# Layer 0's capacity search: seven thresholds tried in one step a turn, in place of three steps of one bit

## The reference

```python
t = B * S                                        # 4096 tokens
probs = softmax(xf @ Wr)                         # 8 experts
topk_probs, topk_experts = top_k(probs, 2)
cap = ceil(t * 2 * 1.25 / 8)                     # 1280
for e in range(8):
    mask = topk_experts == e
    gate = sum(where(mask, topk_probs, 0.0), axis=-1)
    g_masked = where(any(mask, axis=-1), gate, -inf)
    vals, idx = top_k(g_masked, cap)
    g = where(isfinite(vals), vals, 0.0)
    xe = xf[idx]
    y = y.at[idx].add(g[:, None] * (relu(xe @ W1[e]) @ W2[e]))
```

## Time and profile before

| | |
|---|---|
| median of 3 runs | 1777.34 us |
| lowest, highest | 1774.52, 1782.87 us |
| profiled execution | 1775.63 us (span 1773.8 us) |
| TensorE busy, of the span | 1483.0 us (84%), granted clock 0.931 in the mean |
| VectorE busy | 1146.6 us (65%) |
| ScalarE busy | 865.4 us (49%) |
| GpSimd busy | 444.3 us (25%) |

### The profile page before, as it was taken

One profiled execution on the slowest core, in us unless ns is written; L12 is line 12 of the kernel. 1 busy time (PEld: TensorE's weight loads), 2 busy tenths in 40 slices (PEclk: granted clock), 3 DMA queues, 4 the chain that ended last, 5 costly groups with the idle time before them and its releaser, 6 DMA issues.

```text
span 1773.8 us, 40676 instructions
## 1 busy us (share of the span) xinstructions
PE 1483.0 (84%) x11707; PEld 931.5 (53%) x11707; DVE 1146.6 (65%) x3266; ACT 865.4 (49%) x1971; POOL 444.3 (25%) x542
## 2 busy tenths in 40 slices
PE   5355889999998959999995678899999699999997
PEld 4112556666565447778884245455554255555554
DVE  6733566667566847666666456566667577777775
ACT  1012344444443524434441146566665268888787
POOL 3465223223222202222321532112223200000000
PEclk9996899999899969999996589899999789999999
DMA  8442354544443422223320234344442011111110
GB/s 262 129 137 61 106 150 133 180 126 144 145 150 100 123 89 103 96 97 143 132 108 21 98 105 120 96 136 139 139 139 76 23 50 52 51 50 47 47 48 16
DMA packets 127886, 184.90 MB, mean 104 GB/s; under 512 B 14656, under 2 KB 107216, under 8 KB 125344
## 3 DMA queue, kind: packets, MB, share of 16 engines
q1 hardware_dynamic: 94864, 144.54, 25.6%
q10 hardware_dynamic: 26112, 25.17, 4.8%
q0 software_dynamic: 6816, 14.02, 2.2%
HBM read 148.44 MB, written 42.84 MB: 108 GB/s over the span
## 4 chain that ended last, share of the span: by engine, by line
PE 55%; DVE 16%; issue 13%; DMA 6%; ACT 4%; SPq 2%; POOL 2%; another core or an unknown queue 1%; DVEq 1%; ACTq 0%; POOLq 0%
PE pO L777 7%; PE pT_ L634 7%; PE pH L568 6%; PE pH L660 6%; PE pY L668 5%; PE pY L581 5%; DVE mx L1411 3%; PE pS L720 3%; PE pS L742 3%; DMA stk<-packed_qk 2%; ACT pex L894 2%; PE pT_ L632 2%; DVE ob L1507 1%; SPq L1652 1%; DVE wb L1450 1%
## 5 line engine op out<-in xcount | busy, mean ns | idle before, releaser
L894 ACT ACTIVATE pex<-pT_ 128x512 f32<-128x512 f32 (+1 forms) x768 | 427.3, 560 | 485.3 <-PE pT_ L634 306.4
L1411 DVE TENSOR_REDUCE mx<-pS 128x2 f32<-128x512 f32 x512 | 347.8, 689 | 156.3 <-PE pS L611 90.3
L634 PE MATMUL pT_<-stk 32*128 32x256 f16 x1024 | 201.0, 282 | 92.0 <-DMA stk<-packed_qk 31.6
L948 POOL DMA_INDIRECT home_y<-ysb,home x117 | 115.0, 983 | 541.2 <-DVE ysb L1434 281.6
L611 PE MATMUL pS<-stk 32*128 32x256 f16 x1024 | 207.4, 290 | 28.2 <-DVEq L1154 17.5
L777 PE MATMUL pO<-pex,va 128*9 128x256 f32 (+1 forms) x3072 | 201.7, 383 | 2.6 <-ACT pex L894 2.6
L634 PEld LDWEIGHTS pT_<-stk 32*128 32x128 f16 x1024 | 55.5, 93 | 207.7 <-issue 88.4
L887 ACT ACTIVATE wb<-pH,b 128x256 f32<-128x256 f32 x256 | 107.3, 470 | 117.4 <-PE pH L568 117.0
L581 PE MATMUL pY<-wb,w 128*128 128x256 f32 x512 | 131.7, 393 | 12.8 <-DVE wb L1450 12.8
L568 PE MATMUL pH<-XT,w 128*128 128x256 f32 (+1 forms) x512 | 133.1, 388 | 1.0
L660 PE MATMUL pH<-xsT,wb 128*128 128x128 f32 x888 | 132.2, 294 | 0.3 <-ACT xsT L863 0.3
(11 more groups left out here) (226 smaller groups left out, 2548.4 us busy)
## 6 DMA issues: line engine op xcount, KB each, us to landing
wb<-in_w SPq DMA_DIRECT2D x72, 514.0 KB
stk<-packed_qk ACTq DMA_DIRECT2D x96, 256.0 KB, 2.7
wb<-in_w SPq DMA_DIRECT2D x39, 578.0 KB
packed_qk<-qk SPq DMA_DIRECT2D x144, 128.0 KB, 2.0
wb<-gates_turned SPq DMA_DIRECT2D x8, 2048.0 KB, 7.1
pex<-gates_turned SPq DMA_DIRECT2D x8, 2048.0 KB, 7.5
xsb<-sorted_x SPq DMA_DIRECT2D x111, 64.5 KB, 4.1
sorted_x<-in_c_places SPq DMA_DIRECT2D x4, 1548.0 KB, 15.1
```

The lines of the kernel that those rows point to most:

```text
L634: return pe.matmul(bank[:, part * T:(part + 1) * T], key, stk[rows, side, j, 0:T], start=True, stop=True)
L894: ins = act.activation(pex[:, k % 8, 0:n], bank[:, 0:n], ACT.Exp)
L948: pool.indirect_dma_start(YH, bass.IndirectOffsetOnAxis(ap=home[:, place_:place_ + 1], axis=0), ysb[:, place_, :], None).then_inc(sem(f"ho ...
L1411: ins = dve.tensor_reduce(mx[:, :, j, col], bank.rearrange("p (c n) -> p c n", c=2), AX.X, ALU.max)
```

## The change

Each search step now tries seven thresholds in all experts at once, which settles three bits, and a turn does one step instead of three. The number of turns stays 10. The product C stands at step 0 only and sums 56 columns. At step 1 the number of thresholds that are reached is added up and the threshold raised; at step 3 the seven increments are divided by 8 and the next candidates made; at steps 12, 13 and 14 two, two and three of the seven are compared and counted (512, 512 and 768 elements), in the scratch tile `ra`. Every VectorE instruction of the search but the last reduce is now linked, that is waited for at once. Two uses of the S ring a turn are gone. The constant `bitf` has 56 columns instead of 8. `start_search` counts for seven thresholds as well.

```diff
-SEARCH_STEPS, SEARCHES_A_TURN, MARKS_A_SEARCH = 5, 3, 6
-SEARCH_TURNS = range(2, 12)
+SEARCHES, TRIED = SEARCH_BITS // 3, 7
+TRIED_AT_ONCE = (slice(0, 2), slice(2, 4), slice(4, 7))
+SEARCH_AT = {0: ("C", 0), 1: ("c", 1), 3: ("c", 2), 12: ("c", 3), 13: ("c", 4), 14: ("c", 5)}
+MARKS_A_SEARCH = 12
+SEARCH_TURNS = range(2, 2 + SEARCHES)
...
-            if layer == 0 and n in SEARCH_TURNS and h < SEARCHES_A_TURN * SEARCH_STEPS:
-
-                k, part = divmod(h, SEARCH_STEPS)
-                frame += [("c", 10 * k + part) if part else ("C", k)]
+            if layer == 0 and n in SEARCH_TURNS and h in SEARCH_AT:
+                frame += [SEARCH_AT[h]]
...
-        cand = sb("cand", [P, 8], I32)
-        bitf = sb("bitf", [P, 8])
-        biti = sb("biti", [P, 8], I32)
+        cand = sb("cand", [P, TRIED, 8], I32)
+        bitf = sb("bitf", [P, TRIED, 8])
+        biti = sb("biti", [P, TRIED, 8], I32)
         addb = sb("addb", [P, 8], I32)
+        above = sb("above", [P, TRIED, 8])
+        taken = sb("taken", [P, 8])
+        tried = sb("tried", [P, TRIED, 8])
+        cmpt = ra[:, :, :].rearrange("p t e -> p (t e)").rearrange("p (c e t) -> p c e t", c=3, e=8)
...
-                        first = SEARCHES_A_TURN * SEARCH_TURNS[0] - 1
-                        pe.wait_ge(sem("counted"), PRIMED + turn.count(SEARCHES_A_TURN, k - first))
-                        pe.matmul(bank[:, 0:8], onesm[:, :], cnt[:, :], start=True, stop=True)\
-                          .then_inc(s("S_full"), 1)
+                        pe.wait_ge(sem("counted"), PRIMED + turn.count(1, 1 - SEARCH_TURNS[0]))
+                        pe.matmul(bank[:, 0:TRIED * 8], onesm[:, :], tried[:, :, :].rearrange("p c e -> p (c e)"),
+                                  start=True, stop=True).then_inc(s("S_full"), 1)
...
-                chain.link(dve.tensor_copy(biti[:, :], bitf[:, :]))
-                for part in count_parts(chain):
-                    m = part()
-                    if isinstance(m, int):
-                        chain.wait(m)
-
-            def search_parts(c):
-
-                return [
-
-                    lambda bank: c.mark(dve.scalar_tensor_tensor(addb[:, :], bank[:, 0:8], float(CAP), bitf[:, :],
-                                                                 ALU.is_ge, ALU.mult)),
-                    lambda: c.mark(dve.tensor_tensor(thr[:, :], thr[:, :], addb[:, :], ALU.bitwise_or)),
-                    lambda: c.mark(dve.tensor_scalar(bitf[:, :], bitf[:, :], 0.5, None, ALU.mult)),
-                    lambda: c.mark(dve.tensor_copy(biti[:, :], bitf[:, :])),
-                ] + count_parts(c)
-
-            def count_parts(c):
-
-                return [
-                    lambda: c.mark(dve.tensor_tensor(cand[:, :], thr[:, :], biti[:, :], ALU.bitwise_or)),
-                    lambda: c.mark(dve.tensor_tensor(cmp_[:, :, :], key[:, :, :], e_t(cand[:, :].bitcast(F32)), ALU.is_ge)),
-                    lambda: dve.tensor_reduce(cnt[:, :], cmp_[:, :, :], AX.X, ALU.add).then_inc(sem("counted"), 1),
-                ]
-
-            def search(turn, tc, k, bank, s):
-
-                parts = search_parts(tc)
-                if bank is not None:
-                    searched[:] = [parts[0](bank)]
-                    tc.wait(searched[0])
-                    dve.sem_inc(s("S_free"), 1)
-                    return
-                for part in {1: (1, 2), 2: (3,), 3: (4,), 4: (5, 6)}[k]:
-                    if part != 2:
-                        tc.wait(searched[-1])
-                    searched.append(parts[part]())
-
-            searched = []
+                next_thresholds(chain)
+                for part in range(len(TRIED_AT_ONCE)):
+                    count_tried(chain, part)
+
+            def raise_thresholds(c):
+
+                c.link(dve.tensor_reduce(taken[:, :], above[:, :, :].rearrange("p c e -> p e c"), AX.X, ALU.add))
+                c.link(dve.tensor_tensor(addb[:, :], taken[:, :], bitf[:, 0, :], ALU.mult))
+                c.link(dve.tensor_tensor(thr[:, :], thr[:, :], addb[:, :], ALU.bitwise_or))
+
+            def next_thresholds(c):
+
+                c.link(dve.tensor_copy(biti[:, :, :], bitf[:, :, :]))
+                c.link(dve.tensor_tensor(cand[:, :, :], biti[:, :, :], thr[:, None, :].to_broadcast([P, TRIED, 8]),
+                                         ALU.bitwise_or))
+
+            def count_tried(c, part):
+
+                some = TRIED_AT_ONCE[part]
+                n = some.stop - some.start
+                c.link(dve.tensor_tensor(cmpt[:, 0:n, :, :], key[:, None, :, :].to_broadcast([P, n, 8, NT]),
+                                         cand[:, some, :, None].bitcast(F32).to_broadcast([P, n, 8, NT]), ALU.is_ge))
+                ins = dve.tensor_reduce(tried[:, some, :], cmpt[:, 0:n, :, :], AX.X, ALU.add)
+                if part < len(TRIED_AT_ONCE) - 1:
+                    c.link(ins)
+                else:
+                    ins.then_inc(sem("counted"), 1)
...
-                        search(turn, tc, 0, bank, s)
+                        tc.link(dve.tensor_scalar(above[:, :, :].rearrange("p c e -> p (c e)"), bank[:, 0:TRIED * 8],
+                                                  float(CAP), None, ALU.is_ge))
+                        dve.sem_inc(s("S_free"), 1)
+                    elif kind == "c" and k == 1:
+                        raise_thresholds(tc)
+                    elif kind == "c" and k == 2:
+                        tc.link(dve.tensor_scalar(bitf[:, :, :], bitf[:, :, :], 0.125, None, ALU.mult))
+                        next_thresholds(tc)
                     elif kind == "c":
-                        search(turn, tc, k % 10, None, s)
+                        count_tried(tc, k - 3)
...
-    c["c_bitf"] = np.full((P, 8), 2.0 ** (SEARCH_BITS - 1), f)
+    steps = 2.0 ** (SEARCH_BITS - 3) * np.arange(1, TRIED + 1, dtype=f)
+    c["c_bitf"] = np.broadcast_to(steps[:, None], (P, TRIED, 8)).astype(f)
```

More of the change, by code:

```diff
@@ L454, in build @@
                        (tri[:, :], d["c_tri"]), (rope0[:, :, :], d["c_rope0"]),
-                       (rope2[:, :, :], d["c_rope2"]), (bitf[:, :], d["c_bitf"]), (blockno[:, :], d["c_blockno"])],
+                       (rope2[:, :, :], d["c_rope2"]), (bitf[:, :, :], d["c_bitf"]), (blockno[:, :], d["c_blockno"])],
             "ld_1": [(wr[1][:, :], d["wr1"]), (br[1][:, :], d["br1"].partition_broadcast(P)),
@@ L672, in take_turn @@
                     elif kind == "C":
-                        first = SEARCHES_A_TURN * SEARCH_TURNS[0] - 1
-                        pe.wait_ge(sem("counted"), PRIMED + turn.count(SEARCHES_A_TURN, k - first))
-                        pe.matmul(bank[:, 0:8], onesm[:, :], cnt[:, :], start=True, stop=True)\
-                          .then_inc(s("S_full"), 1)
+                        pe.wait_ge(sem("counted"), PRIMED + turn.count(1, 1 - SEARCH_TURNS[0]))
+                        pe.matmul(bank[:, 0:TRIED * 8], onesm[:, :], tried[:, :, :].rearrange("p c e -> p (c e)"),
+                                  start=True, stop=True).then_inc(s("S_full"), 1)
                     elif kind == "U":
-                        pe.wait_ge(sem("counted"), PRIMED + SEARCH_BITS + (2 if k == 0 else 3))
+                        pe.wait_ge(sem("counted"), PRIMED + SEARCHES + (2 if k == 0 else 3))
                         equal = cmp_[:, :, :].rearrange("p e t -> p (e t)")
@@ L1257, in above_capacity @@
             def above_capacity():
-                dve.wait_ge(sem("counted"), PRIMED + SEARCH_BITS + 1)
+                dve.wait_ge(sem("counted"), PRIMED + SEARCHES + 1)
                 chain.link(dve.tensor_tensor(keep[:, :, :], key[:, :, :], e_t(thr[:, :].bitcast(F32)), ALU.is_gt))
@@ L1524, in take_turn @@
                 if l == 0 and turn.n == LOOPS[0][0] - 1:
-                    tc.pad(SEARCHES_A_TURN * MARKS_A_SEARCH)
+                    tc.pad(MARKS_A_SEARCH)
                 tc.leave()
```

## The result

The changed kernel takes 1785.95 us (median; 1775.56 to 1798.90), the kernel before 1778.26 (1771.96 to 1788.46) in the runs beside it: a ratio of 1.0049 [1.0028, 1.007]. It is slower by half a per cent, outside the range of the prediction. The profiled execution took 1789.8 us in all, against the 1775.6 of before. The kernel before itself moves between comparisons (its medians went from 1749 to 1784), so from here on only ratios are compared. Much of that lies near the start: of the kernel after, two profiles of 1788.0 and 1751.8 us differ by 20.4 us (76.6 for 56.2) in the two turns behind the first staging at 105.3 us. What makes the difference there is not known.

What follows compares the result with a forecast made beforehand. In search turns TensorE's standing still or working for the search was taken to count: 1775.6 - 11.0 (structure) + 1.0 (contention) + 1.6 (clock) = 1767.2, and 1768 with half of the median's 1.7 added; range 1756 to 1782 us for 8 in 10.

Steps and rivals of the forecast that it cites:

- The C at step 5: Search turns, step 5: dropping this product and its compare and count gains 1.38 us; idle time 1.10 shrinks to 0.2.
- The new waits: Search turns, steps 14 to 1: TensorE waits 0.8 us at Y5, 0.6 at C, 0.5 at T1.
- A turn without a fall: Search turns, from C at step 0 to the next, clock staying up: 30.6 us, where it lasted 31.7.
- The long operations: VectorE at steps 12 to 14: compare and reduce take 0.69 us over 512 elements, 0.95 over 768.
- The start: Before turn -1: counting seven thresholds takes 3.9 us more, hidden by the stk transfer; turn 0 begins near 103.
- rival 3: At T0: the stk transfer is late in all turns, losing the 1.24 us of steps 9 to 11 ten times; 1780; chance 0.09.
- rival 4: Steps 12 to 14: long counts don't fit, slowed by sharing SBUF with POOL; 1792 at half the doubling; chance 0.10.
- Rival 5: Search turns: five waited marks at 0.11 us each make a turn 0.55 shorter; chance 0.04.
- The clock: Search turns: six falls behind step 5 go, seven behind step 0 come, each 1.6 us; 1.6 lost.
- the sum: Search turns: ten gains of 2.62 us less nine losses of 1.54 and one of 1.3; 11.0 gained.
- Rival 2: Search turns: clock falls in every turn and stays down longer, three more falls and half a dozen us; 1777; chance 0.14.
- Rival 1: Search turns: idle times cut in three don't make the clock fall, seven falls less, 11 us; 1757; chance 0.16.

Runs made afterwards that it cites:

- experiment 7: Changed kernel with the three long counts moved from steps 12, 13 and 14 to steps 3, 4 and 5; ratio 1.0115 to the kernel before.
- filling: Changed kernel with masks and score products repeated at steps 8 to 10 of turn 14; ratios 1.0021 and 1.0012 to the kernel before.
- delay: Changed kernel with 9 more transposes in turn 13, 1.0 us; ratios 0.9989 and 1.0007 to the kernel before.
- experiment 2: Changed kernel with TensorE's three gaps near the new waits filled by repeated products and transposes; ratio 0.991 to the kernel before.

## Why the prediction was wrong

**The structure was right, nearly row by row.** The C at step 5: gain of 1.38 forecast, the idle time of 0.2 is 0.21. The new waits: Y5 0.8, C 0.6, T1 0.5 forecast; 0.84, 0.60 to 0.68 and 0.36 to 0.43 measured. A turn without a fall: 30.6 forecast, 30.96 measured, before 31.7; the 0.3 are more than the 0.1 taken for contention, and with the long operations at their computed length, contention there is not the cause. The long operations: 0.69 and 0.95 forecast, 0.68 to 0.69 and 0.95 measured. The start: turn 0 begins at 103.16 (103 forecast); TensorE waits 6.59 for maxima there, and the transfer of stk hides it:

```profile
74.86 1.20 PE L616 MATMUL pS<-stk 32*128 32x256 f16 x4 [6.59 <-DVE mx L1403]
...
103.16 0.37 PE L639 MATMUL pT_<-stk 32*128 32x256 f16 x1 [8.59 <-DMA stk<-packed_qk]
```

Together 10.0 us forecast; 8.7 to 10.7 at the full clock, which is an upper bound, and near 8.7 in nine turns of the profile (below). Rivals 3 and 4 didn't come in the search: the six long operations cost what they should, and stk is not late in all turns. The compare that took twice the median and that rival 4 went by is this one of before, with what POOL did beside it:

```profile
437.07 0.89 DVE L1238 TENSOR_TENSOR cmp_<-key,cand 128x256 f32<-128x256 f32 x1 [0.33 <-DVE va L1396]
...
436.37 1.29 POOL L1008 TENSOR_TENSOR qkf<-qkf 128x512 f32<-128x512 f32 x1
```

In the search turns the ten compares that lie in a scatter of POOL took 0.46 to 0.49 us, and the ten with nothing of POOL beside them 0.41. The long operations of after have only scatters beside them, for up to 0.87 us, and keep 0.68 to 0.69 and 0.95. Rival 5, with a chance of 0.04, would make a turn 0.55 shorter, by five waited marks at 0.11 each. It is not, and the marks cost the same in the kernel after: a reduce starts 0.04 us behind the compare whose mark is waited for (375.21, behind 374.49 and 0.68), and maxima 0.08 before the end of the last reduce, whose mark isn't (380.87, for 380.00 and 0.95).

**The step that failed is "The clock", in two terms.** First the price of a fall. The number was near (seven forecast behind the pile, five found there), but each was priced 13.76 - 12.20 = 1.6, from the falls behind step 5, and they cost 2.9, as 33.85 - 30.96 shows. The text took the nearest row by the *size* of the idle time (1.10), and took from the T0 at 449.39 only whether a fall follows, not how long it lasts. That row was the nearest by *place*, and its windows (above) give 6.8 us and 2.9. With it the term is 7 x 2.9 in, 6 x 1.6 and that one of 2.9 out: 7.8 lost instead of 1.6, and the forecast 1774, "same". The trace of before had all of that. That it was place that made this row the right one is not shown: experiment 7 has falls of 6.8 away from step 0. In the profile the nine turns behind the staging near 222 us have 16.3 in and 10.9 out (five of 1.6 and the one of 2.9; the sixth of 1.6 stands in front of them): 5.4 lost. They take 295.9 us for 299.2, so without the clock they gain 8.7, of which 1.2 are shorter waits for stk (1.53 for 1.10 and 1.62); the forecast for nine turns is 9 x (2.62 - 1.54 - 0.1) = 8.8.

Second, and larger: the sum ended with turn 12. Every stretch behind the search was taken to last as long as before, only earlier. In the profile turn 14 takes 10.6 more and two turns of layer 2 take 9.3 more, with instructions that the change doesn't touch. For turn 14, filling and delay show that it is the clock; for layer 2 it is a late transfer of stk first, and the clock behind it. That is the wait of rival 3, which was looked for in the search turns and came 600 us behind them. The kernel of experiment 2, with the same instructions there, has its first T0 wait at 0.62 only, and the third profile of the unchanged kernel after has the two at 0.99 and 1.07, so this part is not in every execution; what decides is not shown. No row of before prices this, but a forecast that moves the rest of the program by 10 us, in a kernel with seven falls in its search turns already, needed room for it in its range. In the timed executions turn 14 costs some 4 to 8 us of the clock's 16 to 21 at most. How the others divide between the search turns and layer 2 stays open; so does what makes the transfer late there, and why a fall lasts 3.4, 6.8 or 27.3 us.

Rival 2 was the nearest: the clock low for longer. It had the mechanism (falls longer than before) with another number of them (all ten) and a smaller price (half a dozen us in all; with its three more falls of 1.6 that makes 1779 and not the 1777 given). Rival 1 argued that no idle time under 1.1 is followed by a fall. The profile refutes it: 0.84, 0.68 and 0.36 in a row are followed by one, though not each time, as the choice of seven had assumed.

## What to carry to other kernels

Here, with TensorE busy nine tenths of a turn, idle time was paid twice: as the wait, and in some turns as a fall of the clock behind it. The second payment must be priced by rows of its own: look for every fall in the trace, with how long it lasted and what stood in front of it, and where they differ let the range hold the dearest. Long work of another engine belongs where each piece fits between two waits; a pile of three pieces brought 1.9 us of waits and, where the clock fell, 2.9 more, and the same work in five pieces made the kernel 1.9% faster than before. Behind a change that shifts the rest of a program, compare the untouched stretches too, and give the range room for them.

## What the hardware showed that was not expected

- More work made the program faster: with repeated products in TensorE's gaps, 1.7 us of its time a turn, the ratio is 0.991, without them 1.0033 to 1.0049. The waits in front of a fall were 0.84, 0.68 and 0.36 us, and the same three waits also stood in a turn without one. In front of other falls stands a wait for a transfer instead (1.13 and 1.38 us without any search step).
- The falls that were read lasted 3.4, 6.8 or 27.3 us. In the longest TensorE was busy nearly all the time (1.00 in the windows at 610 and 621) and got no higher clock.
- One microsecond of added work ahead of turn 14 removed a fall of 27.3 us (59.0 for 69.6), with the same waits of 0.55 and 0.70 us in front, and in the kernel before 2.4 us of it made a new one of 3.4.
